# A transformer layer with routed experts: clears in long pieces, scatters in one run, later routing counts, waitless fills in setup, earlier first experts

## What is computed

```
xn  = layernorm(x)
att = softmax(causal(q k^T * 8**-0.5)) v  per head (16 heads of size 8), then @ w_proj + b_proj
      with q, k, v = split(xn @ w_qkv)
gates: logits = xn @ Wg.T (8 experts), the two largest per token, softmax over those two
ffn = sum over the token's two experts e of gate_e * (gelu(xn @ W1[e] + b1[e]) @ W2[e] + b2[e])
out = x + att + ffn            # 4096 tokens, 512 hidden columns per expert
```

## Time and profile before

| what | value |
|---|---|
| median of 3 runs | 753.11 us (751.09 to 756.8) |
| the profiled execution, its own time | 753.37 us |
| its span in the trace | 751.3 us |
| mean granted clock of PE | 0.877 |
| busy: PE, DVE, ACT, POOL | 674.6, 529.0, 442.2, 267.6 us |
| chain that ended last, by engine | PE 67%, DVE 17%, ACT 7%, issue 5% |

### The profile page before, as it was taken

One profiled execution on the slowest core, in us unless ns is written; L12 is line 12 of the kernel. 1 busy time (PEld: TensorE's weight loads), 2 busy tenths in 40 slices (PEclk: granted clock), 3 DMA queues, 4 the chain that ended last, 5 costly groups with the idle time before them and its releaser, 6 DMA issues.

```text
span 751.3 us, 14474 instructions
## 1 busy us (share of the span) xinstructions
PE 674.6 (90%) x4866; PEld 392.8 (52%) x4866; DVE 529.0 (70%) x1797; ACT 442.2 (59%) x656; POOL 267.6 (36%) x431
## 2 busy tenths in 40 slices
PE   6899777989888999989999999988999999999987
PEld 5674333434334655555665555645565555556533
DVE  6758886568575666767667687778668676777676
ACT  4223453445436666757667675767577776677654
POOL 5813146455560423322332323222333233232411
PEclk9555795587758979999999999999899999999989
DMA  6651963033334743626053443535252615340075
GB/s 160 194 113 19 237 170 111 32 88 103 119 83 116 200 149 77 189 59 197 24 126 105 113 125 96 165 82 176 60 137 69 188 44 138 124 117 12 26 185 156
DMA packets 99289, 87.93 MB, mean 117 GB/s; under 512 B 13296, under 2 KB 86704, under 8 KB 99216
## 3 DMA queue, kind: packets, MB, share of 16 engines
q1 hardware_dynamic: 94320, 76.69, 38.1%
q0 software_dynamic: 4544, 9.35, 3.7%
q10 hardware_dynamic: 352, 0.97, 0.6%
HBM read 49.79 MB, written 20.80 MB: 94 GB/s over the span
## 4 chain that ended last, share of the span: by engine, by line
PE 67%; DVE 17%; ACT 7%; issue 5%; another core or an unknown queue 2%; DMA 1%; POOL 0%; ACTq 0%; DVEq 0%
PE ov L923 18%; PE aux L886 15%; PE aux L984 10%; DVE junk L1123 7%; ACT probs L791 3%; PE aux L936 3%; PE sc L906 3%; PE sc L840 3%; PE aux L941 3%; DVE maxes L1121 2%; PE sc L841 2%; PE sc L842 2%; PE aux L964 1%; PE aux L957 1%
## 5 line engine op out<-in xcount | busy, mean ns | idle before, releaser
L791 ACT ACTIVATE probs<-sc 128x1024 f32<-128x1024 f32 (+1 forms) x320 | 287.2, 941 | 194.1 <-PE sc L906 165.4
L1123 DVE CUSTOM_DVE_ANT_0 junk<-aux,cst 128x128 bf16<-128x128 f32 (+3 forms) x512 | 220.3, 486 | 34.6 <-PE aux L886 30.6
L886 PE MATMUL aux<-kT,qT 32*128 32x512 f32 (+3 forms) x768 | 207.0, 461 | 41.0 <-DVE maxes L1123 9.3
L1121 DVE TENSOR_REDUCE maxes<-aux 128x1 f32<-128x512 f32 x256 | 163.3, 683 | 46.0 <-PE aux L886 37.9
L707 POOL TENSOR_SCALAR_AFFINE_SELECT probs<-probs 128x256 f32<-128x256 f32 x224 | 88.4, 408 | 286.5 <-ACT probs L791 281.7
L923 PE MATMUL ov<-probs,v 128*32 128x512 f32 (+3 forms) x1536 | 178.4, 555 | 0.6 <-POOL probs L707 0.5
L886 PEld LDWEIGHTS aux<-kT,qT 32*128 32x128 f32 x768 | 94.0, 205 | 132.2 <-issue 32.9
L906 PE MATMUL sc<-qT,kT 32*128 32x512 f32 (+3 forms) x768 | 146.1, 438 | 5.8 <-DMA qT<-mT 3.3
L722 POOL DMA_INDIRECT ys<-ysb,back x78 | 75.5, 969 | 103.6 <-DVE ysb L1171 58.8
L984 PEld LDWEIGHTS aux<-w2all,hid 128*128 128x128 f32 x624 | 78.5, 198 | 39.2 <-DVE maxes L1121 22.6
L984 PE MATMUL aux<-w2all,hid 128*128 128x128 f32 x624 | 90.6, 290 | 0.3 <-DVE kql L1060 0.3
(11 more groups left out here) (121 smaller groups left out, 604.0 us busy)
## 6 DMA issues: line engine op xcount, KB each, us to landing
w1b<-w_scr SPq DMA_DIRECT2D x39, 512.0 KB, 4.8
w2all<-in_L_ffn_W SPq DMA_DIRECT2D x39, 256.0 KB, 3.2
xs<-ysb SPq DMA_DIRECT2D x13, 387.0 KB, 8.2
kT<-kqh SPq DMA_DIRECT2D x32, 128.0 KB
w_scr<-w1b SPq DMA_DIRECT2D x8, 512.0 KB
qT<-kqh SPq DMA_DIRECT2D x30, 128.0 KB
xrow<-in_L_attn_x SPq DMA_DIRECT2D x7, 512.0 KB, 6.4
xsin<-xs SPq DMA_DIRECT2D x9, 387.0 KB
```

The costliest lines, as they stand in the source:

```text
L791: nc.scalar.activation(probs[:, s % 2, 2 * half:2 * half + 2, 0:cols], pair(part)[:, :, 0:cols], ACT.Exp).then_inc(sc_done, 1)
L886: last_ = nc.tensor.matmul(bank(part)[:, at:at + cols], qT[n % 3][rows, P * i:P * i + P], kT[n % 3][rows, k0:k0 + cols], start=True, stop= ...
L1121: last_ = nc.vector.reduce_max(dst, src, axis=AX.X)
L1123: last_ = nc.vector.tensor_tensor_reduce(out=junk[:, AUXI[part] % 3, at:at + cols], in0=src, in1=cmask[:, W - cols:W], scale=1.0, scalar=L ...
```

## The change

- A clear's piece is laid out so that each partition writes its six rows to consecutive rows of xs, and the constants of the spare rows are numbered to match; six of the 13 clears move into setup behind the second relay, the other seven stand in steps 0 to 3 of unit 0.
- The fills of setup write a half of score bank sc[1] and wait for no aux bank; the block of 6 becomes 28, and ahead of every early maximum but the first stand 2 more. Step 0 of unit 0 gets the aim 4000 like the others.
- Value-gate products 9 to 11 move from the end of setup into steps 0 and 1 of unit 0.
- The prefix product moves from step 3 to step 4 of unit 0, routing steps 5 to 11 to steps 5 to 7.
- The pacing of the scatters goes; all 64 stand in one run behind step 9 of unit 0.
- In unit 3 rows are loaded in step 0, taken in in steps 2 and 3, hidden stands behind step 3 and down in steps 4 to 6.

```diff
--- before.py
+++ after.py
@@ -81,7 +81,6 @@
 NORM_TILES = [range(0, 4), range(4, 8)] + [range(TPB * b, TPB * b + TPB) for b in range(1, B)]
 PIECES = 13
 SCATTERS = (1, 2)
-SCATTER_FROM, SCATTER_STEPS = 8, 24
 VECTOR_NORMS = 3
 BESIDE_M = 3
 ROUTE = 12
@@ -135,11 +134,14 @@
     parts += [("xt", 0), ("warm", -1, -2, 3), ("xt", 1)]
     parts += [("qk", 0, j, c) for c in range(2) for j in range(2)]
     parts += [("relay", 0)] + [("fetch", e) for e in range(E)] + [("relay", 1)]
+    parts += [("clear", i) for i in range(6)]
     parts += [("vg", 0), ("stats", 2), ("vg", 1), ("vg", 2), ("stats", 3), ("norm", 2), ("norm", 3)]
-    parts.append(("warm", -1, 0, 6))
+    parts.append(("warm", -1, 0, 28))
     early = maxima()[:EARLY_M]
     for i, x in enumerate(early):
         parts.extend(AHEAD.get(i, []))
+        if i > 0:
+            parts.append(("warm", -1, i, 2))
         parts.extend(with_negations([x]))
         if i + 1 == HALF_M + 1:
             parts.append(("rows", 0, 0))
@@ -150,17 +152,17 @@
 
 AHEAD = {0: [("xt", 2)], 2: [("xt", 3)], 4: [("stats", 4), ("norm", 4), ("vg", 3)], 6: [("vg", 4)], 7: [("vg", 5)],
          8: [("xt", 4)], 10: [("xt", 5)], 12: [("vg", 6)], 13: [("vg", 7)], 14: [("vg", 8)], 16: [("xt", 6)],
-         EARLY_M: [("xt", 7), ("vg", 9), ("vg", 10), ("vg", 11)]}
+         EARLY_M: [("xt", 7)]}
 
 BESIDE = {
-    (0, 0): [("relay", 2), ("w1", 0), ("clear", 0), ("clear", 1)],
-    (0, 1): [("route", 0), ("route", 1), ("w1", 1), ("clear", 2), ("clear", 3)],
-    (0, 2): [("route", 2), ("route", 3), ("w1", 2), ("w1_out", 0), ("clear", 4), ("clear", 5)],
-    (0, 3): [("route", 4), ("gate",), ("prefix",), ("w1", 3), ("w1_out", 1), ("clear", 6), ("clear", 7)],
-    (0, 4): [("route", 5), ("route", 6), ("w1_out", 2), ("clear", 8), ("clear", 9)],
-    (0, 5): [("route", 7), ("route", 8), ("w1_out", 3), ("clear", 10), ("clear", 11)],
-    (0, 6): [("route", 9), ("route", 10), ("w1", 4), ("clear", 12)],
-    (0, 7): [("route", 11), ("w1", 5), ("w1_out", 4)],
+    (0, 0): [("vg", 9), ("vg", 10), ("relay", 2), ("w1", 0), ("clear", 6), ("clear", 7)],
+    (0, 1): [("vg", 11), ("route", 0), ("route", 1), ("w1", 1), ("clear", 8), ("clear", 9)],
+    (0, 2): [("route", 2), ("route", 3), ("w1", 2), ("w1_out", 0), ("clear", 10), ("clear", 11)],
+    (0, 3): [("route", 4), ("gate",), ("w1", 3), ("w1_out", 1), ("clear", 12)],
+    (0, 4): [("prefix",), ("w1_out", 2)],
+    (0, 5): [("route", 5), ("route", 6), ("w1_out", 3)],
+    (0, 6): [("route", 7), ("route", 8), ("route", 9), ("w1", 4)],
+    (0, 7): [("route", 10), ("route", 11), ("w1", 5), ("w1_out", 4)],
     (0, 8): [("w1", 6), ("w1_out", 5)],
     (0, 9): [("w1", 7), ("w1_out", 6)],
     (1, 0): [("w1_out", 7), ("bias_out",)],
@@ -214,7 +216,7 @@
         if f + 1 < NGRP:
             parts.append(("load_up", f + 1))
     subs = [(b, u) for b in blocks_of(f) for u in range(BK // P)] if f is not None else []
-    step_of = [6, 6, 7, 7, 8, 8] if f == 0 else list(range(2, 8)) if len(subs) == 6 else list(range(1, 9))
+    step_of = [4, 4, 5, 5, 6, 6] if f == 0 else list(range(2, 8)) if len(subs) == 6 else list(range(1, 9))
     for s in range(NS):
         due, late_rows[:] = list(late_rows), []
         group = take(counts(n)[s])
@@ -250,13 +252,13 @@
             parts.append(("project", B - 1, 0))
         if (n, s) in ((2, 3), (2, 7)):
             parts.append(("load_up", 0) if s == 3 else ("load_down", 0))
-        if f == 0 and s == 2:
+        if f == 0 and s == 0:
             parts.append(("load_rows", 0))
         if f == 0 and s in (3, 5, 7, 8):
             parts.append(("reload", (3, 5, 7, 8).index(s)))
-        if f == 0 and s in (4, 5):
-            parts.append(("rows_in", 0, s - 4))
-        if f == 0 and s == 5:
+        if f == 0 and s in (2, 3):
+            parts.append(("rows_in", 0, s - 2))
+        if f == 0 and s == 3:
             for b in blocks_of(0):
                 parts.append(("hidden", 0, b))
                 parts.extend(take(BESIDE_M))
@@ -265,9 +267,8 @@
             parts.append(("load_down", f + 1))
         if nf and s == 6:
             parts.append(("load_rows", nf))
-        step = NS * n + s - SCATTER_FROM
-        if 0 <= step < SCATTER_STEPS:
-            parts.extend([("scatter", 0, 0)] * (TOPK * NT * (step + 1) // SCATTER_STEPS - TOPK * NT * step // SCATTER_STEPS))
+        if (n, s) == (SCATTERS[0] - 1, NS - 1):
+            parts.extend(("scatter", t, k) for k in range(TOPK) for t in range(NT))
         if n == UNITS - 1 and s in (0, 2):
             parts.extend(("fetch_back", b) for b in range(B) if (b > 0) == (s > 0))
         if n == UNITS - 1 and s in (2, 4, 6, 8):
@@ -281,8 +282,6 @@
 
 def aim(n, s):
 
-    if (n, s) == (0, 0):
-        return 0
     return 2900 if n in GROUP_OF else 3300 if n == UNITS - 1 else 4000
 
 
@@ -325,9 +324,7 @@
     parts += [("store", B - 1, 0), ("values", n, NS - 1), ("warm", n, NS, 4), ("evacuate", n, 1), ("turn", n, 1),
               ("warm", n, NS + 1, 4), ("columns", B - 1, 1), ("warm", n, NS + 2, 3), ("project", B - 1, 1),
               ("store", B - 1, 1)]
-    parts = fill(parts)
-    scatters = iter([(t, k) for k in range(TOPK) for t in range(NT)])
-    return [("scatter",) + next(scatters) if x[0] == "scatter" else x for x in parts]
+    return fill(parts)
 
 
 SCHED = schedule()
@@ -358,10 +355,6 @@
 LAST_MAX = {(n, c): max(D_AFTER["max", n, m] for m in (range(HALF_M) if c == 0 else range(HALF_M, NM)))
             for n in range(UNITS) for c in range(2)}
 
-
-
-PACED = {x: [y for y in SCHED[:i] if y[0] == "scores"][-1] for i, x in enumerate(SCHED)
-         if x[0] == "scatter" and any(y[0] == "scores" for y in SCHED[:i])}
 
 
 def both(table, n, s):
@@ -568,7 +561,7 @@
                     i = part[1]
                     sp.wait_ge(zrow_zero, 1)
                     sp.wait_ge(dest_set, 2)
-                    sp.dma_start(xs.rearrange("(g v p) c -> g p v c", p=P, v=SPARE)[i], zrow).then_inc(xs_zero, 16)
+                    sp.dma_start(xs.rearrange("(g p v) c -> g p v c", p=P, v=SPARE)[i], zrow).then_inc(xs_zero, 16)
                 elif what == "rows":
                     n, c = part[1:]
                     sp.wait_ge(aux_a, A_AFTER[part])
@@ -685,8 +678,6 @@
                                             ALU.subtract).then_inc(w1l_done, 1)
                 elif what == "scatter":
                     t, k = part[1:]
-                    if part in PACED:
-                        pool.wait_ge(sc_done, PAIRI[PACED[part]] + 1)
                     if (t, k) == (0, 0):
                         pool.wait_ge(slots_ready, 1)
                         for i, tiles in enumerate(NORM_TILES):
@@ -927,13 +918,16 @@
                 elif what == "warm":
 
                     unit = NEXT_AUX[part]
-                    if unit:
-                        aux_free(unit)
+                    if part[1] < 0:
                         src = kT[0] if part[2] < 0 else wh
                         if part[2] == -3:
                             pe.wait_ge(zeroed, 1)
                         for _ in range(part[3]):
-                            nc.tensor.matmul(bank(unit)[:, 0:FILL], src[:, 0:P], src[:, 0:FILL], start=True, stop=True)
+                            nc.tensor.matmul(sc[1][:, 1, 0:FILL], src[:, 0:P], src[:, 0:FILL], start=True, stop=True)
+                    elif unit:
+                        aux_free(unit)
+                        for _ in range(part[3]):
+                            nc.tensor.matmul(bank(unit)[:, 0:FILL], wh[:, 0:P], wh[:, 0:FILL], start=True, stop=True)
                 elif what == "turn":
                     n, c = part[1:]
                     pe.wait_ge(ot_evac, EVAC["evacuate", n, c] + 1)
@@ -1204,7 +1198,7 @@
     c[:, K_BLK:K_BLK + NBLK] = np.arange(NBLK)
     for k in range(TOPK):
         c[:, K_DEST + NT * k:K_DEST + NT * k + NT] = TOPK * (P * np.arange(NT)[None, :] + np.arange(P)[:, None]) + k
-    c[:, K_DEST + TOPK * NT:] = TOPK * TOK + P * np.arange(SPARE)[None, :] + np.arange(P)[:, None]
+    c[:, K_DEST + TOPK * NT:] = TOPK * TOK + np.arange(SPARE)[None, :] + SPARE * np.arange(P)[:, None]
     return c
 
 
```

## The result

The changed kernel took 795.69 us (median of 5 runs, 794.15 to 800.11) where the kernel before took 753.11 us (median of 5, 751.09 to 758.37): a ratio of 1.059, with a 95% interval of 1.055 to 1.063. The forecast was 743 us with a range of 730 to 758. It is wrong in sign and in size. The changed kernel's profiled execution took 800.11 us with a span of 798.1.

The account below looks back on a forecast made before the run. PE at half clock sets the pace in setup, DVE is nearest the bound in unit 0, units 1 and 2 have no full engine. Setup -9.6, unit 0 +0.2, scatters -0.9 make -10.3 from 753.4: 743 us, range 730 to 758.

Parts of the forecast that it names:

- Scatters: Units 1 to 3: 64 scatters in one run end near 188 us; 0 in units 1 and 2, -0.9 us in unit 3.
- Rival 4: Scatter run in the way, by ports (+2: 745) or stretching past 205 us and holding unit 3's masks (745 to 765); chance 0.05.
- Setup: Before unit 0: fills keep PE busy and the clock full, products move out; first exponential at 48.8 instead of 58.38, -9.6 us.
- Rivals 2 and 3: Setup: clock falls inside it, say near 34 us (748, chance 0.15); level not held, fills dead weight (763, chance 0.12).
- Unit 0: First attention unit: moved products cost, later prefix product gains, clears 0; sum +0.2 us.
- (a): Unit 0, steps 0 and 1: moved value-gate products delay DVE's routing; +1.3 us at full clock, +4.9 at half, +3.1 taken.
- (b): Unit 0, prefix product a step later: its count is long there, so PE need not wait; -2.9 us (0 if DVE idles in step 4).
- Clears: Setup and unit 0: transfers beside DVE's routing, PE waits for none; 0, or +0.5 us if the negated maxima's transfer queues behind.
- Unit 3: No scatters left there: -0.9 us (0 to -2); first experts two steps sooner: 0, with -1 to +1.

Follow-up runs that it names:

- second comparison: Both kernels unchanged, the changed one with products back, the one before with setup's fills alone: before 732.43, changed 722.22 (0.987), products back 720.25, fills alone 728.56 us.
- The run alone: Kernel before with only its scatters made one unbroken run behind unit 0: 729.04 us (0.998) beside a before of 731.73, 803.3 us (1.065) beside 752.39.

## Why the prediction was wrong, point by point

**The step that failed** stands under "Scatters": "GpSimd has nothing else in units 1 and 2, so the pacing cost nothing there". It put taking the pacing away at 0 in units 1 and 2 (and -0.9 in unit 3). That measured +66 in unit 1 in the setting of the first result (and -11 in unit 2, where no scatter is left: 36.80 against 47.80), because the unbroken run holds TensorE's completion signals back, a wait that stands in no term of the sum. Rival 4 had the right place but the wrong reasons and too small a size: it priced the ports (+2) and the run's length past 205 us, 765 at most. The ports bore this out little again: in the changed kernel's profile of the second comparison 31 of the 32 mask clears lie beside scatters, with a median of 0.418 us and at most 0.493. What I should have used stood in the earlier trace rows: three waits of ScalarE with no releaser, 13.8 us, all while scatters were being issued. I wrote that they "may come or go". The question to ask of them was what they had in common, and what the change does to that. Two of VectorE's, 4.0 and 3.7 us, stand in the same stretch of that trace, and the sum, 21.5 us, is near the 20 that these units lose between this kernel's two levels.

A rule of the Trainium skill would have helped to read them, though not to price them: "Perfetto Trace Analysis" (section "Tensor Engine Instruction (MATMUL, LD_WEIGHTS)") says that a matmul's profiled end is an estimate, and that its semaphore update follows later, when PSUM has acknowledged the writes. By that, a reader who waits though PE's bar has ended waits in the gap behind the bar. The trace agrees that there is such a gap: from the row's bar to its copy 0.04 us in one setting, 50 in the other.

**Setup** was right: the first exponential came at 49.6 (predicted 48.8; before 58.38), the clock was 1.00 from 10.60 to 51.60. The 28 fills did not wait:

```profile
18.59 5.06 PE L926 MATMUL sc<-wh 128*128 128x384 f32 x28
23.49 0.60 PE L852 MATMUL aux<-cst,xrow 128*128 128x128 f32 x4
```

Predicted were 18.6, 5.3 us, and transposes 0.7 later than 23.02; they were 0.5 later. The kernel with fills alone starts its first exponential at 52.9: the changed kernel with its products back starts it at 54.3. So the clock gave 4.1 to 5.5 us and the moved products the rest, up to 5.0. Rivals 2 and 3 are out.

**Unit 0** was +0.2 and measured +6.5. Of the 6.3 us between them 2.4 lie in (a), 1.5 in (b) and 2.4 in steps that the sum had at 0. On (a): the clock fell at 51.6, as the sum allowed, and products 9 and 10 began behind the block of maxima, at half clock:

```profile
54.82 0.48 PE L837 MATMUL aux<-wh,xh 128*128 128x136 f32 x1
...
59.79 0.29 DVE L1117 CUSTOM_DVE_ANT_0 junk<-aux,cst 128x128 bf16<-128x128 f32 x1 [3.95 <-PE aux L877]
...
68.67 0.41 DVE L1004 MEMSET attnT<- 128x416 f32 x1 [2.33 <-ACT w2all L756]
```

DVE stands 3.95 us behind the first eighteen and 2.33 us ahead of routing step 0: 6.3 us, where I took 3.1 and 4.9 at most; the second wait holds the 1.66 us that PE waits for a bank ahead of the last six, which the sum didn't have. Steps 0 and 1 grew from 14.9 to 20.4 us. In the prompt setting steps 0 and 1 last 20.37 us with the products and 14.27 without, with DVE busy alike:

```profile
49.30:69.67 20.37, 19.28 (x76) 11.77 (x75) 13.77 (x42) 6.49 (x14) 4.45 (x8) 0.56 0.20 79
```

```profile
54.30:68.57 14.27, 13.12 (x52) 6.17 (x49) 13.96 (x43) 5.00 (x7) 4.86 (x8) 0.68 0.00 1
```

The second line is the kernel with the products back. So the move costs 6.1 and gives 5.0 at the start: it is worth nothing. (b) The wait of PE for the prefix's input is gone as predicted; PE's load there waits for maxima only. Step 3 fell from 7.2 to 5.2 us and step 4 rose from 4.9 to 5.5, so it gave 1.4 of the 2.9. The rest is VectorE's: it still stands idle for 1.79 us, now for the prefix product itself. The other 2.4 us lie in steps 2 and 5 to 8, at other clocks.

**Clears**: nobody waits for them; landing 5.2 us in place of 8.2.

**Unit 3** was better than predicted: 51.70 against 57.2, and 51.7 against 57.1 in the prompt setting, where -0.9 and 0 stood for scatters and experts. The run alone gives 2.2 of it there (54.9), so about 3 are left for the earlier experts and the clock. The clock has a good part in it: with the products back the same unit 3 takes 56.3 us at a granted clock of 0.82, against 0.93. What the earlier experts give is not shown.

Where signals are prompt, the sum came close: -10.2 us measured (722.22 against 732.43), -10.3 forecast. The agreement is partly luck, since in the profiled pair unit 0 was 10.9 us longer and what lies behind unit 4 6.5 shorter (granted clock 0.99 against 0.97), and the sum had neither.

## What to carry to other kernels

A wait for which the profile finds no releaser is a price to be explained before anything near it is changed: look at what all of them coincide with. A pacing that "costs nothing" by the queues may be what keeps the engines' signals moving, so leave time between each two indirect transfers of GpSimd (here 1.0 us behind each 0.97 of issue was enough, 0.5 was not), or issue plain ones where the addresses allow. And where one kernel's time differs by 3% from one comparison to the next, measure a change in both settings: this one is -1.3% in one and +5.9% in the other.

## What the runs showed of the hardware

- In one setting, while GpSimd's indirect transfers ran back to back (0.96 us each, 0.30 between), completion signals of TensorE came only now and then: its readers went on at 141.93, 148.23, 153.84, 158.77, 164.36 and 169.96, and next at 199.44, 8 us behind the run. VectorE's signals to TensorE and ScalarE's to VectorE were prompt (142.52 to 142.57, 154.44 to 154.47). A values product was reported 54 us behind the end of its last matmul, in the other setting 0.05.
- The loss falls with the rest between scatters: units 1 and 2 take 158, 113 and 81 us at one scatter each 1.27, 1.46 and 1.99 us. Plain transfers of 0.54 us, 64 in 38 us, don't show it. Indirect ones in groups lose less than in one run: in twos and threes units 1 and 2 take 102.8 us (81.1 in the prompt setting), in eights 109.8.
- Of six comparisons, four had the slow signals (before at 752.4 to 754.0) and two did not (731.7 and 732.4); it held for all runs of a comparison. One chip number stood over a comparison of either kind, so the number alone doesn't decide. What does, and by which path the signals are held, no run here shows.
- The setting can be told from a trace, whatever the kernel. PE's products change one semaphore 795 times in each of these kernels; the eight traces of the prompt setting have 792 to 796 records of it, the twelve of the slow-signal one 760 to 789. Records of VectorE's and ScalarE's semaphores are fewer too (959 and 502 instructions; 940 and 489 records in the first result, 976 and 506 in the same kernel in the prompt setting). So in a slow-signal trace a wait under "issue" may belong to a late signal too. Whether these records and the delays have one cause isn't shown.
